# Spreading the gates of two expert units by two matrix products of 64 rows each, in a one-core language-model tower on Trainium2

## The reference, cut to what matters

```python
E, K, D, H, DOUT = 8, 2, 64, 128, 64
xn = (x - mu) * rsqrt(var + EPS) * gamma + beta                  # (8, 512, 64)
logits = xn @ Wr + br                                            # (8, 512, 8)
top_vals, top_idx = top_k(logits, 2)
w = softmax(top_vals)
w_full = sum over k of w[..., k] * one_hot(top_idx[..., k], 8)   # the gates, (8, 512, 8)
for e in range(8):
    h = gelu(xn @ W1[e] + b1[e])                                 # (8, 512, 128)
    y = y + (h @ W2[e] + b2[e]) * w_full[..., e, None]
return x + y                                                     # x is the input of this layer
```

## Time and profile before

| what | value |
|---|---|
| time, median of 3 runs | 432.4 us (427.66, 432.4, 433.17) |
| the profiled execution's own time | 430.44 us |
| its span, first to last instruction | 428.7 us |
| PE busy | 394.7 us, 92% of the span |
| DVE busy | 348.2 us, 81% |
| ACT busy | 326.7 us, 76% |
| POOL busy | 270.7 us, 63% |
| mean granted clock of TensorE | 0.973 of full speed |

### The profile page before, as it was taken

How to read it: one execution, slowest core, us unless ns; L and a number is a source line. 1 busy time by engine, 2 the same in 40 slices (tenths; PEclk the granted TensorE clock), 3 DMA queues, 4 the chain that set the end, 5 groups by cost and what they waited for, 6 DMA issues and landing times.

```text
span 428.7 us, 6335 instructions
## 1 busy us (share of the span) xinstructions
PE 394.7 (92%) x2000; PEld 320.4 (75%) x2000; DVE 348.2 (81%) x809; ACT 326.7 (76%) x557; POOL 270.7 (63%) x436
## 2 busy tenths in 40 slices
PE   5687799999999999999999999888888998999996
PEld 2575578888888888888888887776666766877884
DVE  4898788889888898888888778788775779989773
ACT  1264788999999998889878636468756989989993
POOL 0556777877778788787775554776334766444542
PEclk9899999999999999999999979899988999999998
DMA  6800003221222211222120000000000000000001
GB/s 208 335 2 0 1 27 49 51 46 32 48 49 51 45 33 50 49 51 41 35 49 26 1 2 1 1 2 2 0 0 2 0 2 13 12 15 12 14 12 25
DMA packets 15834, 14.94 MB, mean 35 GB/s; under 512 B 9781, under 2 KB 10553, under 8 KB 15545
## 3 DMA queue, kind: packets, MB, share of 16 engines
q1 hardware_dynamic: 15800, 14.54, 14.0%
HBM read 13.42 MB, written 1.11 MB: 34 GB/s over the span
## 4 chain that ended last, share of the span: by engine, by line
PE 71%; DVE 10%; ACT 9%; issue 3%; DMA 3%; POOL 2%; SPq 1%; POOLq 0%; DVEq 0%
PE ps L1425 64%; PE ps L1448 4%; DMA hh<-in_tokens 3%; ACT ezf L791 2%; ACT hid L854 2%; ACT w_all L860 2%; DVE stats L934 1%; DVE hh L1214 1%; PE ps L1456 1%; SPq L387 1%; PE ps L1655 1%; PE ps L1611 1%; SPq L391 1%; PE ps L1721 1%; ACT scratch L756 1%
## 5 line engine op out<-in xcount | busy, mean ns | idle before, releaser
L670 ACT ACTIVATE hid<-ps,b_fold 128x512 f32<-128x512 f32 x128 | 84.0, 681 | 21.2 <-PE ps L1425 20.8
L1006 DVE TENSOR_TENSOR hid_lo<-hid,hid_hi 128x1024 fp32r<-128x1024 f32 x64 | 78.6, 1229 | 25.3 <-ACT hid_hi L675 25.1
L1425 PE MATMUL ps<-xn_hi,w_all 128*128 128x512 f32 x256 | 87.4, 402 | 1.2 <-DVE xn_lo L1001 1.2
L1425 PE MATMUL ps<-hid_hi,w_all 128*128 128x512 f32 x256 | 85.0, 393 | 0.0
L675 ACT ACTIVATE hid_hi<-hid 128x1024 fp32r<-128x1024 f32 x64 | 67.9, 1061 | 2.0
L1425 PEld LDWEIGHTS ps<-xn_hi,w_all 128*128 128x128 f32 x256 | 48.4, 189 | 11.3 <-issue 1.4
L1425 PEld LDWEIGHTS ps<-hid_hi,w_all 128*128 128x128 f32 x256 | 48.1, 188 | 9.9
L1425 PE MATMUL ps<-xn_lo,w_all 128*128 128x512 f32 x128 | 49.9, 390 | 0.0
L1425 PE MATMUL ps<-hid_lo,w_all 128*128 128x512 f32 x128 | 49.8, 389 | 0.0
L854 ACT ACTIVATE hid<-ps,eb_fold 128x512 f32<-128x512 f32 x64 | 44.1, 689 | 1.6 <-PE ps L1425 1.2
L1425 PE MATMUL ps<-hid_hi,ew 128*128 128x512 f32 x128 | 42.6, 416 | 0.6 <-ACT hid L854 0.2
(11 more groups left out here) (228 smaller groups left out, 907.6 us busy)
## 6 DMA issues: line engine op xcount, KB each, us to landing
rstd_row<-roots SPq DMA_DIRECT2D x29, 256.0 KB, 4.0
hh<-in_tokens SPq DMA_DIRECT2D x8, 256.0 KB, 8.2
hid<-in_w SPq DMA_DIRECT2D x1, 1024.0 KB, 7.6
rstd_row<-in_w SPq DMA_DIRECT2D x1, 1024.0 KB, 10.6
out<-hh SPq DMA_DIRECT2D x8, 128.0 KB, 2.0
ew_raw<-in_expert_w SPq DMA_DIRECT2D x1, 512.0 KB, 10.0
roots<-rstd SPq DMA_DIRECT2D x29, 2.0 KB, 1.4
ew_raw<-in_expert_w SPq DMA_DIRECT2D x1, 256.0 KB, 10.0
```

Source lines behind the costliest of these rows:

```text
L670: act.activation(hid[:, j % 2, f, :], bank[f], ACT.Gelu, bias=b1_fold[:, j // B * F + f:j // B * F + f + 1]).then_inc(gelu_done, 1)
L1006: dve.tensor_tensor(hid_lo[:, j % 2, 2 * p:2 * p + 2, :], hid[:, j % 2, 2 * p:2 * p + 2, :], hid_hi[:, j % 2, 2 * p:2 * p + 2, :].bitcast( ...
L1425: return pe.matmul(out, lhsT, rhs, start=start, stop=stop)
```

## The change

From unit 18 on, the gates of an even unit n and of n+1 are spread together, at the place where the even one's product stood; the odd unit's place is empty. Each of the two products has 64 rows: the even unit uses partitions 0 to 63 of both operands, the odd one partitions 64 to 127. For that the gates and the 0/1 matrix stand twice: `sel_pair` holds the first half of the matrix in both halves, and `gates_out` copies columns 0 to 15 of each block of `w_pad` (8 high and 8 low parts) to columns 64 to 79, so that the transpose puts them at partitions 64 to 79. The pair waits once, for the bank of the odd unit, that is for `dve_job(n - 2)`. Units 0 to 17 are as before. There are 23 pairs.

```diff
+        sel_pair = sb("sel_pair", [P, E], fp32r)
...
             def gate_rows():
                 own.inc(dve.tensor_copy(sel[:, :], cons[:, K_SEL:K_SEL + E]))
+                own.inc(dve.tensor_copy(sel_pair[0:P // 2, :], cons[0:P // 2, K_SEL:K_SEL + E]))
+                own.inc(dve.tensor_copy(sel_pair[P // 2:P, :], cons[0:P // 2, K_SEL:K_SEL + E]))
...
                 chain(dve.tensor_copy(parts[:, :, :, 0:E].bitcast(fp32r), twice))
-                dve.tensor_tensor(parts[:, :, :, E:2 * E].bitcast(fp32r), twice, parts[:, :, :, 0:E],
-                                  ALU.subtract).then_inc(gates_ready, 1)
+                chain(dve.tensor_tensor(parts[:, :, :, E:2 * E].bitcast(fp32r), twice, parts[:, :, :, 0:E],
+                                        ALU.subtract))
+                dve.wait_ge(pad_zeroed, 1)
+                dve.tensor_copy(w_pad[:, r, P // 2:P // 2 + 2 * E].bitcast(fp32r),
+                                w_pad[:, r, 0:2 * E]).then_inc(gates_ready, 1)
...
+            def spread_gates_of_two(n):
+
+                pe.wait_ge(hw_ready, last_use(n + 1, spread_bank) + 1)
+                for k in (n, n + 1):
+                    part = slice(k % 2 * P // 2, (k % 2 + 1) * P // 2)
+                    mm(bank[spread_bank(k)], sel_pair[part, k % E:k % E + 1].broadcast_to([P // 2, P]),
+                       row_of(wT_all, k)[part, :]).then_inc(wb_done, 1)
...
-                    spread_gates(n)
+                    if n <= 2 * E + 1:
+                        spread_gates(n)
+                    elif n % 2 == 0:
+                        spread_gates_of_two(n)
```

## The result

The changed kernel took 434.2 us (median of 5 runs, 433.22 to 437.56); the kernel before, timed with it, 429.68 us. The ratio is 1.012, with a 95% interval of 1.0075 to 1.0165: slower by 4.5 us by the medians and by 5.2 by the ratio, within 2%. Ratios are taken over executions that are not in the slower state of the chip that a few of them fall into. The forecast was 439.0 us, 1.5% slower than 432.4; it starts from the median of three executions, and with five that median is 429.68. So 2.7 of the 4.8 us between forecast and result are the starting point's, and 2.1 the change's. The profiled execution took 434.2 us against 430.44, with a span of 432.4 us against 428.7.

What follows compares the result with a forecast made beforehand. PE was taken to bound the expert units after row 3 of the loop; 4.9 + 0.2 + 1.1 + 0.33 + 0.5 = +7.0 us on 432.4 gave 439.4, rounded to 439.0 us; range 432.5 to 443.5.

Steps and rivals of the forecast that it cites:

- What bounds the kernel: In the expert units, after row 3 of the loop, a cost on PE is paid in full.
- The switch: On PE, going to fewer rows and back loses 0.20 us each way, 0.40 us a pair.
- Rival (b): At PE's pairs no switch is paid: -0.23 us a pair, about -3.2 in all, 429.2 us; chance 0.15.
- The overlap: Inside a pair on PE, the second load follows 0.11 us after the first, giving back 0.13; a pair costs +0.27 us.
- My lower bound of +0.17: Cost of a pair on PE in us if the two weight loads also coincide.
- How many pairs are paid: Units 24 to 34 and 40 to 62: 18 pairs at 0.27, 4.9 us; pairs 18, 20, 22 together 0.2.
- The bank wait: At unit 38, in row 4, PE waits for DVE: 1.1 us; free in rows 5 to 7, nothing added around 26.
- The copies: Three more DVE copies in `gates_out`: +0.33 us in the first group, 0.2 and 0.3 reaching PE from the others.
- The fear that they would wait for POOL: In the other two groups of `gates_out`, the new DVE copy may wait for POOL, taking 0.2 to 1.2 us each.
- The range: Whole kernel: 432.5 to 443.5 us.
- rival (c): Switches paid but loads coincide, +0.17 a pair, row 4 stall absorbed: +4.3 us, 436.7 or less; chance 0.15.
- the stall of row 4: PE's wait on DVE at the pair of unit 38, forecast at 1.1 us with semaphore time.

Runs made afterwards that it cites:

- e5: The changed kernel with each 64-row product in its own unit's place, with the old wait, instead of paired: ratio to the kernel before 1.0272, loop time 107.8 us.
- e6: The changed kernel with products of 32 rows in place of 64: ratio to the kernel before 1.0077, loop time 97.5 us.
- e1: The changed kernel with both products of a pair at all 128 rows: ratio to the kernel before 1.0049, loop time 95.6 us.
- e3: The changed kernel with both products of a pair on partitions 0 to 63: ratio to the kernel before 1.0203, loop time 100.9 us.
- e8: The changed kernel with each pair issued one unit later, at the odd unit's place: ratio to the kernel before 1.0049, loop time 96.9 us.
- e4: The kernel before with only the earlier bank wait added, from unit 18 on: ratio to the kernel before 1.0014, loop time 94.9 us.
- e7: The changed kernel itself, timed again on another occasion: ratio to the kernel before 1.0094, loop time 97.4 us.

## Why the prediction was right or wrong

**What bounds the kernel.** Right: PE leads rows 5 to 7, and each cost on it there is paid in full (row 6: 4 pairs x 0.16 = 0.64 for 0.6 measured; ten pairs at 0.16 from unit 44 on; e5: 0.40 a visit). The warning that DVE leads around the third group's gate steps was in the same paragraph, and I used it too little, see below.

**The switch.** Right, to the hundredth: 0.40 us for two, from matrix products of another type and size. e5 shows it alone, e6 that 32 rows cost what 64 do, e1 that it goes when the height is full. Rival (b), no switch between fp32r products, is out. That the 0.20 us of each switch are an emptying of PE (0.10) and an open load (0.10) was a reading of rows that fits all of these; no run takes the two apart.

**The overlap.** This is one mis-sized term. I took the loads one after the other, 0.11 us apart, and +0.27 a pair; they go at once, and a pair costs +0.16. My lower bound of +0.17 was this case. I had read two loads 0.11 apart in the trace, but both of them went to the same rows. For 18 pairs the difference is 18 x 0.11 = 2.0 us. e3 shows the overlap from the other side.

**How many pairs are paid.** The other mis-sized term. At 0.16 each the 18 pairs would be 2.9 us; the loop shows 1.8. By the table it is the place that counts: the ten pairs of units 44 to 62 are paid in full, and of the eight others that the forecast counted, units 24 to 34, 40 and 42, almost nothing reaches DVE. PE does lose the time there: counted from the loop's start, its hidden product of unit 35 comes 0.57 us later than in e1. But DVE and its gate steps lead behind it, and at unit 37 only 0.20 of it is left. I added the terms as if they lay one behind the other, yet where PE waits for DVE anyway, a switch ahead of the wait costs nothing more. e8 fits: with the bank wait gone, the loss up to unit 43 is still 1.0 us beside the copies, as with it. That in e8 it is the switches that fill this 1.0, and not DVE's later gates, was argued and not tested.

**The bank wait.** 1.1 us were forecast and e4 has 1.2, but that is luck in the larger part. The forecast put all of it at unit 38 and nothing at 26, since DVE's lag wouldn't grow with PE's. In e4 0.7 us are there by unit 37 (by unit 29 already), before that place, from the waits at units 22 and 26 (0.26 and 0.48 us in the changed kernel; what PE loses at 20 is caught up by its product of unit 22). Unit 38 and its neighbours, where PE stands longest, give the other 0.5, and only behind unit 43, when PE leads again.

**The copies.** 0.5 us in the loop where I had 0.5 for these two with what they push, and 0.33 ahead of it, which neither times nor profiles can confirm, since the start of the loop varies by more. The fear that they would wait for POOL didn't come true; for the last copy the rows show that POOL was done when it began, since the old copy ahead of it had ended with POOL's subtraction.

**The sum.** 1.8 + 1.2 + 0.5 + 0.2 = 3.7 us in the loop, against 7.0 with 0.33 ahead of it. The times say 4.1 (e7) to 5.2 us; the 0.4 to 1.5 us beyond the loop's are within what the way before the loop varies by. The range held the result, the direction and "within 2%" were right, and the size of the change was too high by about 2 us by the times and 3 in the loop, for the reasons above; the median of 432.4 that it was added to was too high by 2.7 more. The changed kernel ended nearest to rival (c), +4.3 us, and for one of its two reasons: the loads coincide. Its other one, that the stall of row 4 is absorbed, is half borne out: 0.5 of 1.1 us stay. But it has 3.1 us for pairs where 1.8 were paid, and nothing for the 0.7 us of waiting at units 22 and 26. That it came close in all is partly these misses cancelling.

## What to carry to other kernels

Where PE sets the pace, a visit to less than full row height amid full-height products cost two switches here, 0.40 us at the full clock, whether it held one product or two; two on separate halves took the time of one. As an estimate from these numbers, with 512 columns, break-even is at 0.40 / 0.233 + 1, or about 2.7 full products replaced by a visit. A pair doesn't reach it; four spread at once might, if the banks were there and if four overlapped as two do, which no run shows. When an edit both adds work to one engine and makes it wait earlier for another, don't add the two where they meet in the same gap: take the longer, and keep the sum as the upper bound. And follow the loss unit by unit in the trace, against the kernel before: two totals can agree, 1.1 and 1.2 us here, and come from different places.

## What the runs showed of the hardware that was not expected

Weight loads onto separate row halves start together: two loads in 0.19 us, where two loads to the same rows take 0.29 (e3's pair, which differs from the changed kernel's in just that). The first record behind each switch is 0.10 us longer than a full one's 0.39, 0.49 for a 64-row product and 0.50 for the full one that follows, which fits a load that lies open in it. And the way before the unit loop, the same for all kernels but for DVE's copies, ended between 324.3 and 331.7 us in ten profiles, with mean granted clocks between 0.965 and 0.991 (the latest start had the lowest clock, e4): 7.4 us, twice what the change costs in the loop.
